# A two-layer GNN block: products and aggregations turned, GCN order exchanged, tiles of 125 nodes

## The reference

```python
deg_inv = 1.0 / maximum(segment_sum(ones, dst), 1.0)
h   = relu(x @ W_self0 + (A_in @ x) * deg_inv @ W_neigh0 + b0)
out =      h @ W_self1 + (A_in @ h) * deg_inv @ W_neigh1 + b1
y   = layernorm(x + out)
# GCN with self loops, row = src, col = dst
g   = y @ W_gcn.T + b_gcn
norm = deg_row[row] ** -0.5 * deg_row[col] ** -0.5
result = layernorm(y + segment_sum(norm * g[col], row))
```

## Time and profile before

| | |
|---|---|
| median of 3 runs | 964.1 us (963.81 to 964.86) |
| the profiled execution | 968.54 us, of which the span from first to last instruction is 966.8 us |
| instructions | 11088 |
| PE busy | 868.5 us, 90% of the span |
| DVE, ACT, POOL busy | 375.0, 121.6, 405.7 us |
| HBM read, written | 104.08 MB, 64.53 MB |
| mean granted TensorE clock | 0.962 of full speed |

### The profile page before, as it was taken

How to read it: one execution, slowest core, us unless ns; L and a number is a source line. 1 busy time by engine, 2 the same in 40 slices (tenths; PEclk the granted TensorE clock), 3 DMA queues, 4 the chain that set the end, 5 groups by cost and what they waited for, 6 DMA issues and landing times.

```text
span 966.8 us, 11088 instructions
## 1 busy us (share of the span) xinstructions
PE 868.5 (90%) x3926; PEld 718.3 (74%) x3926; DVE 375.0 (39%) x581; ACT 121.6 (13%) x132; POOL 405.7 (42%) x330
## 2 busy tenths in 40 slices
PE   0699999399990599979999999999999999999996
PEld 0488888378870488868888888887888888888885
DVE  0756666001110377742222522223656433334545
ACT  0411114000000010102111400000111111110000
POOL 0078788577577687787776861000000000000000
PEclk9999999799995699989999999999999999999999
DMA  9644459967741588646446855655765311214543
GB/s 353 233 131 132 140 182 316 334 193 223 210 111 23 142 239 230 194 113 207 131 132 197 284 175 204 204 200 166 246 237 185 118 55 45 86 35 142 182 171 108
DMA packets 97331, 169.40 MB, mean 175 GB/s; under 512 B 15762, under 2 KB 62604, under 8 KB 97300
## 3 DMA queue, kind: packets, MB, share of 16 engines
q1 hardware_dynamic: 64212, 110.65, 35.9%
q10 hardware_dynamic: 22800, 57.82, 15.7%
q0 software_dynamic: 10288, 0.54, 3.0%
HBM read 104.08 MB, written 64.53 MB: 174 GB/s over the span
## 4 chain that ended last, share of the span: by engine, by line
PE 57%; POOL 18%; issue 13%; DVE 6%; DMA 4%; ACT 1%; SPq 0%; ACTq 0%; POOLq 0%; DVEq 0%
PE acc L834 34%; PE acc L874 20%; POOL adj_in L407 18%; PE turned L803 2%; DMA bias<-in_src 2%; DVE in_part L634 2%; PE acc L856 1%; DVE outb L732 1%; DVE dpart L646 1%; ACT w_hi L453 1%; DVE w_lo L548 1%; DMA adj<-adj_in 1%; DMA outb<-in_L_gnn_W_neigh 1%; DVE outb L736 0%; DMA xin<-h_scr 0%
## 5 line engine op out<-in xcount | busy, mean ns | idle before, releaser
L834 PE MATMUL acc<-w_hi,xt_hi 128*128 128x512 f32 x800 | 251.5, 396 | 21.3 <-DMA xt_lo<-xt_lo_scr 15.7
L834 PE MATMUL acc<-w_hi,xt_lo 128*128 128x512 f32 x800 | 250.0, 394 | 0.0
L407 POOL DMA_INDIRECT adj_in<-mult,idx_in x160 | 203.1, 1269 | 110.9 <-issue 110.9
L834 PE MATMUL acc<-w_lo,xt_hi 128*128 128x512 f32 x800 | 238.9, 390 | 0.0
L407 POOL DMA_INDIRECT adj_out<-loops,idx_out x160 | 199.2, 1245 | 67.0 <-issue 63.3
L874 PE MATMUL acc<-u_hi,adj 128*128 128x512 f32 x580 | 183.9, 399 | 38.4 <-DMA adj<-adj_in 36.2
L834 PEld LDWEIGHTS acc<-w_hi,xt_hi 128*128 128x128 f32 x800 | 150.1, 190 | 52.4 <-issue 15.9
L874 PE MATMUL acc<-u_lo,adj 128*128 128x512 f32 x580 | 181.7, 395 | 0.0
L834 PEld LDWEIGHTS acc<-w_lo,xt_hi 128*128 128x128 f32 x800 | 150.5, 188 | 31.8
L834 PEld LDWEIGHTS acc<-w_hi,xt_lo 128*128 128x128 f32 x800 | 150.7, 190 | 31.1
L874 PEld LDWEIGHTS acc<-u_hi,adj 128*128 128x128 f32 x580 | 110.2, 192 | 61.8 <-DMA adj<-adj_in 36.6
(11 more groups left out here) (83 smaller groups left out, 330.9 us busy)
## 6 DMA issues: line engine op xcount, KB each, us to landing
adj<-adj_in SPq DMA_DIRECT2D x20, 640.0 KB
xt_hi_scr<-xt_hi ACTq DMA_DIRECT2D x20, 512.0 KB
xt_lo_scr<-xt_lo ACTq DMA_DIRECT2D x20, 512.0 KB
xt_hi<-xt_hi_scr SPq DMA_DIRECT2D x20, 512.0 KB
xt_lo<-xt_lo_scr SPq DMA_DIRECT2D x20, 512.0 KB
self_scr<-outb ACTq DMA_DIRECT2D x20, 512.0 KB
xin<-self_scr SPq DMA_DIRECT2D x20, 512.0 KB
xin<-y_scr SPq DMA_DIRECT2D x20, 512.0 KB
```

Source lines behind the costliest of these rows:

```text
L407: pool.indirect_dma_start(table, bass.IndirectOffsetOnAxis(ap=index[0:EP, j:j + 1], axis=0), counts[0:EP, j:j + 1], None, bounds_check=CEL ...
L834: ins = nc.tensor.matmul(acc[:, s, cols], left[:, s, k * P:(k + 1) * P], right[:, k, cols], start=(i == 0), stop=(i == len(steps) - 1))
```

## The change

All tiles have T = 125 rows (1250 = 10 x 125), and everything that is moved or cleared by nodes has 125 partitions. The adjacency tables are laid out as five panels of 250 columns.

- The first self product (`self_turned`) and the first aggregation (`mean0`) make their result transposed: weights or u are the stationary operand with 128 columns, nodes are the moving one, in chunks of 500, 500, 250 and of 250, 500, 250, 250 columns. h comes out already transposed, so that the products of layer 1 load it (`load_tile`) and the PE transposes no tile there.
- The GCN aggregates first (`gather`, transposed, chunks of 250, 500, 250, 250) and multiplies by the weight after.
- The first aggregation waits for the scatters that its destination chunk needs (`NEEDS`), not for all.
- The loads of edge numbers go over ACT's queue, by way of a padded copy in DRAM; each table is cleared in four writes of 125 rows x 12500 bytes, both from ACT's queue.

The core of the diff:

```diff
+T = 125
+    CHUNKS = ((0, 2), (2, 4), (6, 2), (8, 2))
+    CHUNKS0 = ((0, 4), (4, 4), (8, 2))
+    NEEDS = (3, 7, 9, GROUPS)
...
+            for i, ids in enumerate((dst, src)):
+                act.dma_start(edges_scr[i, WINDOW:WINDOW + E].rearrange("(p c) -> p c", c=EC), ids.rearrange("(p c) -> p c", c=EC)
+                              ).then_inc(edges_copied, 16)
...
+            act.wait_ge(edges_copied, 32)
+            act.wait_ge(edges_pad, 16)
+            for i, where in enumerate((e_dst, e_src)):
+                windows = bass.AP(tensor=edges_scr.tensor, offset=i * PAD_E, ap=[[RUN, T], [RUN * T, GROUPS], [1, HALO]])
+                act.dma_start(where[0:T, :, :], windows).then_inc(edges_in, 16)
...
+            def turn_hi(t):
+                act.wait_ge(xt_turned, t + 1)
+                if t >= 2:
+                    act.wait_ge(xt_stored[t % 2], 16 * (t // 2))
+                nc.scalar.activation(xs[:, t % 2, 0, 0:KD * T].rearrange("p (b f) -> p b f", b=2), ps[:, 4:6, 0:4 * T], ACT.Copy
+                                     ).then_inc(xt_hi_done, 1)
+            def store_turned(t):
+                act.wait_ge(xt_lo_done, t + 1)
+                act.dma_start(xt_scr[t, :, :, :], xs[:, t % 2, :, 0:KD * T].bitcast(F32)).then_inc(xt_stored[t % 2], 16)
+            def clear(table, done):
+                act.wait_ge(zeros_ready, 1)
+                runs = table.rearrange("(p a j) o -> a p (j o)", a=4, j=ZERO_RUN)
+                for a in range(4):
+                    act.dma_start(runs[a, :, :], zeros).then_inc(done, 16)
+            turn_hi(0)
+            for k in range(KD):
+                split_hi(N0, k)
+                if k == 3:
+                    clear(adj_in, cleared_in)
+            store_turned(0)
+            for t in range(NT):
+                if t + 1 < NT:
+                    turn_hi(t + 1)
+                    evict_hi(N0, t)
+                    store_turned(t + 1)
...
+                if t == 2:
+                    clear(adj_out, cleared_out)
...
+            turn_lo(0)                       # DVE
+            for k in range(KD):
+                split_lo(N0, k)
...
+            edge_keys()
+            edge_cells()
+            edge_form()
+            repeats(0)
...
+            for t in range(NT):              # SP, MEAN1
+                sp.wait_ge(acc_full, acc_index(S1, NT - 2) + 1 if t == 0 else acc_index("MEAN1", t - 2) + 1 if t < 9 else
+                           acc_index("MEAN1", 6) + 1)
+                table = adj_in[t // 2 * PANEL:(t // 2 + 1) * PANEL, :].rearrange("(k p j) o -> p k (j o)", p=T, j=PW)
+                sp.dma_start(p1_tile[t].bitcast(F32), table[:, :, t % 2 * T:(t % 2 + 1) * T]).then_inc(p1_full[t], 16)
...
+                sp.dma_start(xin[0:T, t % 2, :], s1_scr[t * T:(t + 1) * T, :]).then_inc(res_full[t % 2], 16)
...
+            def self_turned():               # PE
+                for i, (c, k) in enumerate(S0_STEPS):
+                    width = CHUNKS0[c][1] * T
...
+                        for left, right in ((0, 0), (0, 1), (1, 0)):
+                            ins = nc.tensor.matmul(ps[:, d, 0:width], w[:, k, left, d * P:(d + 1) * P],
+                                                   where[:, right * BANK:right * BANK + width],
...
+                        for k in range(NT):  # mean0, for each chunk c and each of 8 blocks d
+                            for h in range(2):
+                                ins = nc.tensor.matmul(ps[:, h_bank(m), 0:width].rearrange("p (n j) -> p n j", j=PW),
+                                                       typed(u[0:T, k, h, d * P:(d + 1) * P], exact), typed(panels[:, k, :, :], exact),
```

More of the change, by code:

```diff
@@ L6 @@
 P = 128
-PSUM_COLS = 512
+T = 125
+BANK = 512
 WINDOW = 48
@@ L24, in build @@
     E = src.shape[0]
-    NT = -(-N // P)
-    LAST = N - (NT - 1) * P
+    NT = N // T
     KD = D // P
[L28 to L51, removed]
+    EC = E // T
+    GROUPS = NT
+    RUN = EC // GROUPS
+    HALO = RUN + 2 * WINDOW
+    PW = 2 * T
+    PANEL = N * PW
+    PSIZE = NT * PW
+    CELLS = N * N
+    PER = NT * T
+    PAD_E = E + 2 * WINDOW
+    KEY_LOAD, PAIR_KEYS = 1000, 8
+    WIDE = 4 * T
+    assert N == NT * T and D == KD * P and E == EC * T and EC == GROUPS * RUN
+    assert N < KEY_SHIFT - 1 and SKIP > CELLS and WIDE <= BANK and KD == 8 and NT == 10
+    CHUNKS = ((0, 2), (2, 4), (6, 2), (8, 2))
+    CHUNKS0 = ((0, 4), (4, 4), (8, 2))
+    NEEDS = (3, 7, 9, GROUPS)
+    LATE_K = (4, 5, 6, 7, 0, 1, 2, 3)
+    BLOCK_ORDER = (4, 5, 6, 7, 0, 1, 2, 3)
+    N0, S0, N1, S1, GCN = range(5)
     with ExitStack() as ctx:
@@ L189, in build @@
         norm_done = sem("norm_done")
-        eps_ready = sem("eps_ready")
-        sources = {NEIGH0: x, MEAN0: self_scr, NEIGH1: h_scr, SELF1: x, MEAN1: self_scr, GCN_LIN: y_scr, GCN_AGG: y_scr}
-        made_by = {MEAN0: SELF0, NEIGH1: MEAN0, MEAN1: SELF1, GCN_LIN: MEAN1, GCN_AGG: MEAN1}
-        results = {SELF0: self_scr, MEAN0: h_scr, SELF1: self_scr, MEAN1: y_scr, GCN_AGG: out}
-        weights = [w_neigh0, w_self0, w_neigh1, w_self1, wt_scr]
-        biases = {SELF0: b0, SELF1: b1, GCN_LIN: b_gcn}
@@ L198, in is_end @@
-        def is_end(q, t):
-            return q == GCN_AGG and isinstance(t, int) and t == NT - 1
-        def rows(t):
-            return LAST if isinstance(t, int) and t == NT - 1 else P
-        def tiles(eng, body):
-            with eng.Fori(0, PAIRS - 1) as i:
-                for s in range(SLOTS):
-                    body(i * SLOTS + s, i, s, i * SLOTS + s)
-            for s in range(SLOTS):
-                body(NT - SLOTS + s, PAIRS - 1, s, None)
-        def raw_slot(l, c):
-            return c % (2 * SLOTS) if l in (LIN[NEIGH0], LIN[SELF0], LIN[SELF1]) else c % SLOTS
@@ new lines, in _ @@
+            with pe.Else():
+                mean0(False)
+            for t in range(NT):
+                linear(N1, t)
+            for t in range(NT):
+                linear(S1, t)
+                if t >= 2:
+                    turn_weights(t - 2)
+            with pe.If(general > 0):
+                mean1(True)
+                gather(True)
+            with pe.Else():
+                mean1(False)
+                gather(False)
+            for t in range(NT):
+                linear(GCN, t)
```

1398 lines of the change are left out of this document (847 added, 551 removed).

## The result

| | before | after |
|---|---|---|
| median of the runs, us | 964.4 (963.8 to 964.9) | 1178.0 (1173.7 to 1179.2) |
| ratio, 95% interval | | 1.221 (1.217 to 1.224) |
| span of the profiled execution, us | 966.8 | 1177.2 |
| busy time of PE, us | 868.5 | 933.3 |

The sign was right, the size was half of what came: 1065 had been forecast, within 960 to 1140.

A forecast was written before the change was run, and what follows sets the result against it. The kernel was taken as PE-bound with some 52 us of holes, and 125-row transfers as using five DMA engines. 966.8 + 86 - 60 - 5 - 6 + 11 + 58 + 16 = 1067, so median 1065 us, range 960 to 1140.

The forecast's parts named there:

- NEIGH0 to 241: Start to end of NEIGH0, 154.8 us before: later second tile, holes of 21 and 39 behind the clears; +86.
- MEAN1 152: MEAN1, 93.7 us before: five engines need 15.5 a tile against PE's 9.1, so loads set the pace; +58.
- The last product and tail 121: GCN product after its aggregation, 109 + 2 us, then 8 as before plus 1.5 for the last store on 5 engines.
- The last aggregation, 111: `gather`: PE work 90.7 us, 12 for the first panel and 8 for the two of the wide chunk.
- SELF0 110: SELF0, 170.0 us before: 107 of matmuls and 3 for first loads, waits for scatters and transposed tile gone; -60.
- MEAN0 99.4: MEAN0, 104.5 us before: 96.4 of matmuls plus 3 for row fetches behind two panels in SP's queue; -5.
- NEIGH1 and SELF1 233: NEIGH1 109 plus 2 for weight slices, -6; SELF1 109 + 7 for weights and 6 for crowded engines, +11.
- The clock: 2 us in the sum: In NEIGH0, 2 us were added for a lower PE clock after the hole.
- Hidden transfers (893): Rival: 125-row transfers use 16 engines or enough of them, so no hole is left; 893 us, chance 0.14.
- Stores not held up by the clears (1005): Rival: ACT's queue lets stores pass the clears, so NEIGH0's holes of 21 and 39 go; 1005 us, chance 0.11.
- A narrow product at the price of a wide one: Rival: matmuls of 250 columns cost as much as wide ones, 132 us more; 1197 us, chance 0.05.
- Pieces of 500 bytes paid twice: Rival: MEAN1's adjacency loads double because of 500-byte pieces, 68 us more; 1133 us, chance 0.05.

The follow-up runs named there:

- the run with the panels alone: The changed kernel with only the panels of MEAN0 and `gather` issued as two transfers, of 112 and 13 rows; 1131.1 us.
- The run with the order alone: The changed kernel, row counts kept, with SP's queue order altered so that first tiles of SELF0, NEIGH1 and SELF1 load earlier; 1164.2 us.
- the one with the row tiles alone: The changed kernel with only MEAN1's adjacency tiles and the row tiles (s1, residual x, y, output) issued in 112 + 13 rows; 1097.8 us.
- the 950 us version: The changed kernel with all 125-row transfers in 112 + 13 rows, SP's and NEIGH0's order altered, clears issued in quarters; 950.0 us, 0.983 of the kernel before.
- The split: The changed kernel with every 125-row transfer issued as two, of 112 and 13 rows; 1008.3 us, 1.041 of the kernel before.

## Why the prediction was wrong

The direction and the main mechanism were right: 125 rows go on five engines, and the holes of NEIGH0 and the pace of MEAN1 come from it. Three steps failed. MEAN0 was given "plus 3" for its panels, which cost 22. The seams before NEIGH1 and SELF1 were put at nothing and cost 25. And the lower clock was priced at 2 us in one stage, where it slowed the matmuls of every stage with waits, by some 50 us of PE's busy time. In detail, with the stages as the prediction cut them (span, forecast to measured):

- **NEIGH0 to 241: right in size, and in mechanism for the larger hole.** Its last matmul starts at 234.3. Holes were forecast at 21 and 39 us; they were 14.9 and 34.3, and the second tile started at 65.7 for 71. The second hole ended as foretold, with a store behind the clear. The first was to end with a store too; it ended with an x tile (L1054 in the waits), which shares the clear's five engines.
- **MEAN1 152: 150.1. Right in mechanism, and in the total by luck.** Its tiles are 14.4 us apart for 15.5, so the last one ends some 10 us early; the rest of the 150.1 is 8.4 us for the aggregation's first panel, which the prediction had booked at the aggregation.
- **The last product and tail 121: 122.2. Right.** The last aggregation, 111: 120.6, without the 8.4 us just named. Its other waits for panels, 6.4 and 7.8 us, make 22.6 with it, near the 20 given; PE's work was too low, 90.7 us for 103.2, at a mean granted clock of 0.89.
- **SELF0 110: 126.4.** The step "3 for its first loads" failed: 6.8 us, as those loads stood behind four weight loads in SP's queue, which in turn waited for NEIGH0's last tile. The gap before MEAN0, 5.9, was in no term: 4.3 us of branch, then a panel. The rest is the clock and 0.227 for a chunk of 500, not 0.222.
- **MEAN0 99.4: 143.6, the largest miss.** "Plus 3, since the row fetches stand behind two panels" was the only cost of the panels. The prediction prices a panel of 11 us at `gather` and gives no reason why it costs less here; all of them, and the fetches behind them, need the same five engines in a stage that also writes h in short pieces. It cost 22 us, by the run with the panels alone. Then come 3.3 us for a late degree row, 7.0 of the seam to NEIGH1, and slower matmuls.
- **NEIGH1 and SELF1 233: 279.7.** The prediction has no word on SP's in-order queue at the seams, past which the change moves the loads of both stages: 7.0 us, counted in MEAN0, and 18.3 here. The run with the order alone shortened the two stages by 25, the one with the row tiles alone by 27, the 950 us version by 36. Five engines at "about 13 against 11.7" a tile in SELF1 was too low: tiles 4 to 8 took 13.6 to 15.7. And the product was priced at 0.227, not 0.232.
- **The clock: 2 us in the sum, some 50 in the kernel** (within the misses above, not beside them). The changed kernel and the 950 us version run the same 4402 recorded matmuls; PE is busy for 933.3 us in the one and 882.3 in the other. Of its busy time 129 us lie in stretches at the lower clock in the one and 32 in the other; matmuls there take nearly twice as long (below), so about half of the difference, 49 us by this estimate, is the clock. A short wait is paid again in the slow matmuls behind it. MEAN1's second tile, just after a wait of 5.9 us and a little later:

```profile
799.80:801.50 1.70, 1.70 (x4) 1.41 (x5) 1.13 (x1) 0.54 (x1) 0.00 (x0) 0.50 0.32 133
804.00:806.00 2.00, 2.00 (x10) 1.59 (x9) 0.00 (x0) 0.00 (x0) 0.00 (x0) 1.00 0.33 130
```

  Eight matmuls follow 0.43 us apart on average at the lower of the two clock levels (granted 0.50, 1.2 GHz), the rest 0.226 to 0.239 apart at the upper one (2.4 GHz). In MEAN1 this is mostly hidden, since the loads set the pace; how much of the 50 us reached the total was not measured.

The misses add up: -6 + 16 + 44 + 47 - 2 + 10 + 1 = 110 us, 1067 to 1177. Slips of the working are small beside them: 1069 x 0.9954 is 1064, not 1065; the clear of `adj_out`, 119 + 65, ends at 184, not 186; the DMA share in the earlier trace rows goes down to 0.44, not 0.55; and PE is idle for 32 us of the start, which "nearly all of every stage but one" passes over.

**The rivals.** Hidden transfers (893): fallen. Stores not held up by the clears (1005): fallen, `turn_hi` stood 46 us for a store. A narrow product at the price of a wide one: fallen, 250 columns follow 0.117 us apart on average. Pieces of 500 bytes paid twice: fallen; they took 27 ns each, 1000 bytes 46 ns, and MEAN1 with 16 engines is bound by PE with the very same pieces. All of the surprise lay in the forecast itself, in terms that it set at 6 us or less, or at nothing.

**The rule of engines.** The split's engine counts were taken from the Trainium skill, "DMA: Bandwidth & Descriptors", section "Why a DMA increments its semaphore by 16 and not by 1": 16 divides 112, and 13 is used whole. By that rule, the runs agree: a store at the end has 5 small packets in 125 rows and 29 = 16 + 13 in 112 and 13, and in MEAN1 the two queues go from 27.0 + 9.7% of 16 engines over 150 us to 56.4 + 16.7% over 93, with the same pieces.

## What to carry to other kernels

Count the rows of every transfer before tiling by anything but 128: 125 rows cost this kernel 170 us, and two issues of 112 and 13 rows in place of one of 125 gave them back. Where a table is cleared, spread the issues too. Where a stage starts, read the in-order queue of the engine that loads for it, and put its first tile ahead of whatever waits for the last tile of the stage before. When PE gets short waits, price each one together with the slow matmuls behind it, and don't expect a crowded DMA engine to delay only the transfers that crowd it.

## What the runs showed of the hardware

- Issuing is not free when the engines are behind: the eight transfers of a clear held ACT's queue for 15.5 to 18.5 us, one store of a tile 14.9 us behind a clear on five engines. Alone, such a store is issued in 0.5 us.
- A transfer of 125 rows puts 5 small packets on its queue, the same in 112 and 13 rows 29 = 16 + 13; in MEAN1 with 125 rows, all on the same five engines, the DMA share stands at 0.3 of 16.
- A stationary operand whose slices start at multiples of 500 bytes makes a matmul of 512 columns take 0.232 us in place of 0.227, measured with 125 columns; at 512-byte steps 125 and 128 columns take the same.
- With MEAN1's waits of 2.5 to 5.9 us went stretches of 3.4 to 6.8 us at the lower clock; after its two waits of 2.1 us the clock stayed at its upper level.
- Transfers of 128 rows come late too when they stand behind transfers on five engines: the issue of one fetch of SELF0's result behind three panels took 11.1 us in place of 1.7, and such fetches held DVE for 26.2 us in MEAN0.
- A compare-and-branch of PE took 3.4 to 8.4 us here and ended 1.3 to 1.5 us after a 16 KB packet of the instruction queue; the load of the flag took 0.5 us.
